# Attention rows: twelve spare bf16 products of TensorE behind each block's sums

## The reference

```python
Q, K, V = projections of the normalised nodes (plus the query embedding), 4 heads of 64
mod_k  = K[src] + 0.2 * rel_w[edge_relations][:, None, :]
scores = jnp.einsum('ehd,ehd->eh', Q[dst], mod_k) / D ** 0.5
w      = exp(scores - max over the edges of the same dst) / their sum
agg    = jax.ops.segment_sum(w[:, :, None] * V[src], dst, num_segments=N)
```

## Time and profile before

| | |
|---|---|
| median of three runs | 6448.35 us (6441.57 to 6476.74) |
| the profiled execution | 6469.34 us |
| its span, from the first to the last instruction | 6467.6 us |
| the stage of the change | from about 2085 to 3770 us |

### The profile page before, as it was taken

The page is one execution under the profiler, slowest core; times in us unless marked ns, Lnnn a source line. Parts: engine busy times, 40 slices in busy tenths (PEclk is TensorE's granted clock), DMA queues, the critical chain, the costliest instruction groups (busy, mean ns, idle before and its releaser), DMA issues. The chain is left out here.

```text
span 6467.6 us, 70480 instructions
## 1 busy us (share of the span) xinstructions
PE 4520.9 (70%) x20233; PEld 3157.2 (49%) x20233; DVE 3488.0 (54%) x7038; ACT 1793.7 (28%) x5528; POOL 3336.7 (52%) x2377
## 2 busy tenths in 40 slices
PE   3677787796785566666666647524992699998978
PEld 3455565474562344444444423312651477776446
DVE  8574764743616577777677656750114444443245
ACT  0232332332321355555455420001220112211122
POOL 0011686786887666666666658656545344441000
PEclk9888998898898677777767768656996899999989
DMA  6999312213213666665555124225992455553000
GB/s 227 310 360 298 79 2 53 49 2 79 18 2 71 183 183 175 181 172 166 165 154 167 44 63 133 78 60 180 310 275 66 179 192 191 195 203 138 1 24 20
DMA packets 776171, 881.42 MB, mean 136 GB/s; under 512 B 392349, under 2 KB 645312, under 8 KB 771496
## 3 DMA queue, kind: packets, MB, share of 16 engines
q1 hardware_dynamic: 348392, 633.65, 28.8%
q0 software_dynamic: 417328, 235.13, 17.8%
q10 hardware_dynamic: 10128, 8.79, 0.4%
HBM read 682.29 MB, written 240.09 MB: 143 GB/s over the span
## 5 line engine op out<-in xcount | busy, mean ns | idle before, releaser
L735 POOL DMA_INDIRECT pairs<-REC,FARC x800 | 1684.4, 2106 | 954.9 <-DMA pairs<-REC,FARC 481.7
L1015 PE MATMUL a_pa<-a_VW,identf 128*128 128x260 f32 x1920 | 742.7, 546 | 54.0 <-issue 45.1
L913 POOL DMA_INDIRECT a_KV<-kv_tab,KEYS x600 | 606.6, 1011 | 328.0 <-issue 168.3
L1015 PEld LDWEIGHTS a_pa<-a_VW,identf 128*128 128x128 f32 x1920 | 496.3, 271 | 200.4 <-issue 85.7
L1003 PE MATMUL a_pq<-QS,a_ohT 128*128 x720 | 162.6, 344 | 509.0 <-issue 231.3
L913 POOL DMA_INDIRECT XN<-kv_tab,KEYS x360 | 361.9, 1005 | 272.9 <-ACT a_VW L977 170.4
L2283 DVE TENSOR_TENSOR AIN<-AIN,w_pin 128x512 f32<-128x512 f32 (+1 forms) x325 | 216.5, 666 | 429.4 <-PE w_pin L2322 424.0
L977 ACT ACTIVATE a_VW<-a_KV,a_VW 128x64 f32<-128x64 f32 x1800 | 446.2, 335 | 5.0
L1003 PEld LDWEIGHTS a_pq<-QS,a_ohT 128*128 128x128 bf16 x720 | 77.1, 107 | 635.2 <-issue 614.7
L1700 PE MATMUL m_bank<-m_QK,m_VX 128*128 128x320 f32 x1280 | 359.2, 440 | 3.6 <-ACT m_QK L1590 3.6
L1691 PE MATMUL m_bank<-m_VX,m_QK 128*128 128x256 f32 x1600 | 352.1, 381 | 2.5 <-ACT m_QK L1596 2.5
(11 more groups left out here) (564 smaller groups left out, 9463.2 us busy)
## 6 DMA issues: line engine op xcount, KB each, us to landing
pairs<-ZERO SPq DMA_DIRECT2D x32, 5000.0 KB, 40.5
e_W<-in_L_ffn_w SPq DMA_DIRECT2D x192, 512.0 KB
REC<-pairs SPq DMA_DIRECT2D x100, 800.0 KB, 7.1
RES<-pairs SPq DMA_DIRECT2D x13, 3200.0 KB
HB<-pairs SPq DMA_DIRECT2D x12, 3200.0 KB, 10.3
m_crow<-cell_tab SPq DMA_DIRECT2D x75, 488.3 KB
row_tab<-a_arow SPq DMA_DIRECT2D x240, 130.0 KB
n_AR<-row_tab SPq DMA_DIRECT2D x30, 1040.0 KB, 5.2
```

The lines of the kernel that those rows point to most:

```text
L735: pool.indirect_dma_start(self.pairs[half], bass.IndirectOffsetOnAxis(self.FARC[:, i:i + 1].bitcast(I32), 0), self.REC[:, i, 0:4].bitcast( ...
L913: pool.indirect_dma_start(KV[t % UB][:, j, :], None, self.kv_tab, bass.IndirectOffsetOnAxis(self.SIDX[:, t * ROW + j:t * ROW + j + 1], 0), ...
L1015: last = pe.matmul(sums[b], self.identf[:, :], VW[:, b, e, :, :], start=e == 0, stop=e == ROW - 1)
```

## The change

It adds a PSUM bank, `spare`, and behind the sums of each block twelve products of the bf16 identity with the first 256 columns of `QS` into it. Nothing reads the bank, and no wait or signal is added. The twelve stand in TensorE's stream between line 1015 of block t - 3 and line 1003 of block t + 1, in the blocks that have sums: 240 times 12.

```diff
@@ -860,7 +860,7 @@
-        HV = 1
+        HV, WARM = 1, 12
@@ -875,6 +875,7 @@
             pa = [pb(f"pa{b}", [P, 512]) for b in range(2)]
+            spare = pb("spare", [P, 512])
@@ -1014,6 +1015,8 @@
                                 last = pe.matmul(sums[b], self.identf[:, :], VW[:, b, e, :, :], start=e == 0, stop=e == ROW - 1)
                             last.then_inc(s_a, 1)
+                            for _ in range(WARM):
+                                pe.matmul(spare[:, 0:D], self.identb[:, :], QS[:, 0, 0, :], start=True, stop=True)
                     steps(pe, RB, UB, 3, step)
```

## The result

The changed kernel takes 6555.51 us, the median of four runs (6553.09 to 6568.67), beside 6459.93 (6441.57 to 6476.74) for the kernel before on the same chip: a ratio of 1.0159, 95% interval 1.0133 to 1.0184. It is slower by 96 us between the medians, 103 by the ratio. The profiled execution took 6553.09 us. In what follows "spares" are the added products. The stage's lines are those of before plus one, up to line 1016 (the sums); the spares are line 1019.

A forecast was written before the change was run, and what follows sets the result against it. It took the stage to be bound by TensorE's late reports during POOL's gathers, no engine being full. Spares' time and code at 0 plus 150 us for added rests: 6469 + 150 = 6619 profiled, 6600 for the median; range 6435 to 6750.

The forecast's parts named there:

- The cycle of late reports: Changed stage: POOL gathers, TensorE's reports fall behind, DVE and ACT stand, POOL runs out of buffers and rests; 84 rests.
- The 420 us above 1241: Changed stage: 240 undisturbed blocks at DVE's 5.17 us want 1241 us; some 420 us are something else, put down to standstills.
- Ten microseconds after the products on which they wait had been issued: Standstill at 2719.93: DVE and ACT woke together this late, 1.8 us after POOL's last gather.
- The number of instructions, not their time or clock: TensorE's stream: a block's instructions grow from 46 to 70, delaying reports; more rests, chance 0.51, own range 6520 to 6720.
- The mis-sized term: POOL's added rests: half of 44 at 6.2 us, +136 us, or all at 3.9, +170; taken as +150 us.
- a fixed number of instructions: Rest cycle: each lets 131 TensorE instructions through, so 2.85 blocks become 1.88 and rests go from 84 to 128.
- a fixed stretch: Rest cycle: each lasts a stretch of time after POOL's restart, so the number of rests hardly moves; cost 0.
- The spares lie between a block's sums and the products for which DVE waits.: TensorE's stream: reports come in program order, so the awaited report is one of 54 instructions instead of 30; some cycles lose a block.
- Costed at nothing: Spares' own TensorE time, 4.3 us a block at full clock under DVE's 5.17, and their instruction code: both 0.
- Faster, by the clock: Rival: spares hold TensorE's full clock, sums behind standstills take 2.02 us instead of 3.83; 151 us gained, 6297; chance 0.12.
- Slower by TensorE's own time: Rival: 58% of blocks stay at half clock and cost 7.5 instead of 5.17 us; 320 us lost, 6768; chance 0.17.
- half-clock block that the rival feared: TensorE's block with spares at half clock: 7.5 us, over DVE's 5.17 by 2.3; rival's chance 0.17.

## Why the prediction was right, and where its steps were not

It said slower, 6600 us, between 6435 and 6750; it is 6555.51. The mechanism it named is in the main the one that the runs show, and the size is about two thirds of what it took. The range was wide enough to hold a slight gain as well as a loss three times the measured one, so that it holds the result says little; the runs with other numbers of spares say more.

- **The cycle of late reports.** Right. POOL's rests and the stage move together over four kernels: 256, 324, 410 and 510 us of rests (30, 46, 70 and 94 instructions of TensorE a block), for stages of 1603, 1661, 1752 and 1846 us. The difference is 1336 to 1348 us in each, POOL's own pace.
- **The 420 us above 1241.** Only in part the standstill. The prediction measured the stage against DVE's 5.17 us a block and overlooked that POOL, with indirect gathers, needs some 5.5. So 324 of the 420 us are rests behind late reports and the other 96 are POOL's pace; without indirect gathers both go, and the stage takes 1246 to 1250 us.
- **"Ten microseconds after the products on which they wait had been issued."** Misread by two: the additions' products were issued 12.4 us and the sums 12.0 us before; 11.8 and 10.0 us is since they were over.
- **The number of instructions, not their time or clock.** Right as far as the runs reach, from three sides: 16 columns cost what 256 do, six of 512 what six of 16 do, and without the gathers all twelve are free. Over all but the two with six spares and the one with paired products, the price is 14 to 18 ns for each instruction of the stage (52 us / 3840, 89 and 103 / 5760, 95 / 5760, 195 / 11520). This is an average over blocks with and without a standstill.
- **The mis-sized term.** The prediction took half of 44 added rests at the full rest's 6.2 us, 136 us, or all at 3.9, 170. By the same waits there are 16 more (100 for 84, the scatter's 23 among them) at 4.10 us each, 66 us, and the 84 others grew by 0.24 us, 20 us: 86. A cycle lets through 70 x 240 / 100 = 168 instructions now and let through 131 before, so it is neither a fixed number of instructions (which asked for 128 rests) nor a fixed stretch (84). The choice between these ends was one error. The other is the unit: the loss is the rests' whole time and not their number. The prediction expected 105 to 128 rests; the change has 100, the twelve of 16 columns 87 at nearly the same loss, and the twenty-four 103 at twice the loss.
- **"The spares lie between a block's sums and the products for which DVE waits."** This reason for the choice isn't borne out. Put ahead of the sums they cost 95 us all the same. And in the cycle shown the spares that creep stand behind the awaited products and not ahead of them; what counts, it seems, is how much follows them. In the two cycles shown, their report came with 52 and 55 instructions of TensorE behind it. The Trainium skill ("TensorE: Matmul & The Clock Gate", "Part 2: What happens when you issue a matmul") gives TensorE a window of 64 instructions for pulling weight loads ahead. 52 and 55 would fit a queue of that depth that has to move on before an old report gets out, but the page doesn't say so and no run here varied the depth. If it is so, a block of 46 instructions leaves the reports of more than one block due in the queue, one of 70 less than one; that is argued, not shown.
- **Costed at nothing.** The spares' own time: right, the stage is 1249.6 us without them and 1249.8 with them where no gather is indirect. The code: 22 packets more in the whole program, no wait put down to them, and free where no gather is indirect. Whether TensorE's code comes late while gathers are indirect no run tells.
- **Faster, by the clock.** It had 0.12. The clock did rise (0.71 to 0.82), the sums behind a standstill did not always profit (3.83 us in the block at 2738.36, at 0.57), and at 0.94 against 0.82 without gathers the stages are equal to 0.2 us. In the cycles shown the wait ahead of a restart is the report's.
- **Slower by TensorE's own time.** It had 0.17. Down: with a sixteenth of the columns it should have gone, and it didn't. In the stretch where the twelve took 6.6 us TensorE stood idle for 4.0 of them, by the rows' own waits.

The half-clock block that the rival feared is in the trace:

```profile
2738.36:2745.34 6.98, 6.98 (x37) 5.08 (x36) 6.48 (x12) 5.93 (x25) 2.58 (x3) 0.57 0.35 107
```

TensorE is busy all 6.98 us of it, more than a block's 5.17, and yet DVE's next addition followed its predecessor after 5.58 us (2737.78 to 2743.36). Its relation products (2736.78 to 2738.43) stand ahead of the half-clock sums in TensorE's stream and were over 4.9 us before the addition. That is the lead that the prediction said might absorb it.

What stays open: why indirect gathers hold up TensorE's reports and plain transfers from the same engine do not; whether it is the products, their weight loads or their code that count; why six spares cost a third of their share; and why the paired products gained nothing. Indirect gathers of consecutive rows would separate the indexing from the scattered reads; they were not run. Mixing indirect and plain transfers, or gathers of another size, was not tried. Of the versions with the whole computation none beat the kernel before.

## What to carry to other kernels

Before adding spare work "because the engine has room", look at what the engine's completions are waiting in line with: here twelve matmuls that nobody reads, 1.47 us a block of an engine with 2 us to spare, cost 96 us. Where consumers show "remote" waits while the producer had long been done, count instructions, not their time, and look at what another engine does in that stretch. Ask also which engine sets the pace between the waits: here it was POOL, and only what lengthened its rests cost time. A better clock is worth something only where the wait that ends last is the engine's own time.

## What the runs showed of the hardware that was not expected

- While POOL's indirect gathers follow each other, TensorE comes at times to start one instruction in 0.7 or 1.4 us, whatever it is (0.27 us of work in the change, 0.17 with 24 spares of 16 columns). Its reports come 9 to 12 us after the work in the cycles shown. The first 7 to 9 us of a run of gathers pass without it there (2702.77 to 2710.07 before, 2720.54 to 2729.45 after).
- The end of it isn't always the end of the gathers. Of DVE's 36 waits for late reports in the kernel before, 25 ended 1.1 to 3.7 us behind the last gather of a run and 11 while a gather was under way. Of the 67 in the changed kernel 26 ended 0.9 to 3.3 us behind a run, the others during a gather or within 0.3 us of its end.
- Plain DMAs into the same slots, from SyncE or POOL, at 245 GB/s for 155, do nothing of the kind: 5.22 us a block for 6.95, 6.4% of the whole program, of which POOL's faster pace is a part.
- An indirect gather takes POOL 1.00 us and follows the last by 1.30; four plain transfers of 256 KB took it 2.12 us in most blocks.
- A drain of POOL behind four gathers takes 3.1 us in the mean beyond their rows, 5.2 at most.
- TensorE's mean clock in the stage can be moved from 0.71 to 0.84 by spare products (and from 0.82 to 0.94 without gathers) with no gain in time.
